# Two transformer layers with routed experts: the order of indirect transfers, of the ternary layer and of the experts' rows

## The reference

```python
x = x + L0_attn(layernorm(x))   # 16 heads of 16, rotary, causal window of 128, softmax, output projection
x = x + L0_ffn(layernorm(x))    # softmax router over 8 experts, the best 2 per token, renormalised gates;
                                # expert: silu(a) * b with (a, b) = x @ Wl1[e] + bl1[e] (512 + 512), then @ Wl2[e] + bl2[e]
x = x + L1_attn(layernorm(x))   # 16 heads, xpos rotation, biases, full causal softmax, output projection
x = x + L1_ffn(layernorm(x))    # ternary weight: clip(round(w / s), -1, 1) * s, s = mean(|w|)
```

## Time and profile before

| | us |
|---|---|
| median of three runs | 3257.35 |
| lowest, highest | 3247.95, 3259.71 |
| profiled execution, its own time | 3238.48 |
| its span | 3236.8 |
| PE busy | 2606.6 (81%) |
| DVE busy | 1855.1 (57%) |
| ACT busy | 1375.3 (42%) |
| POOL busy | 922.1 (28%) |
| mean granted clock | 0.900 of 2.4 GHz |

### The profile page before, as it was taken

How to read it: one execution, slowest core, us unless ns; L and a number is a source line. 1 busy time by engine, 2 the same in 40 slices (tenths; PEclk the granted TensorE clock), 3 DMA queues, 4 the chain that set the end, 5 groups by cost and what they waited for, 6 DMA issues and landing times. The chain is left out here.

```text
span 3236.8 us, 51965 instructions
## 1 busy us (share of the span) xinstructions
PE 2606.6 (81%) x17726; PEld 1745.3 (54%) x17726; DVE 1855.1 (57%) x6538; ACT 1375.3 (42%) x2419; POOL 922.1 (28%) x862
## 2 busy tenths in 40 slices
PE   3788888888888399989899952788888888888887
PEld 2455555555555277778777851344444444444444
DVE  3767766775675344444444443666666666666661
ACT  1445544554554233333333311255555545555554
POOL 2434544544342200000000004343333333334300
PEclk8889988988899699999999975799999989999998
DMA  4565565565433565566666544334444433333330
GB/s 118 164 199 169 190 202 166 166 210 194 145 126 99 186 239 212 214 217 215 214 214 214 215 137 117 102 102 123 131 120 128 122 106 106 106 105 111 100 93 14
DMA packets 263344, 494.65 MB, mean 153 GB/s; under 512 B 27104, under 2 KB 194272, under 8 KB 253024
## 3 DMA queue, kind: packets, MB, share of 16 engines
q1 hardware_dynamic: 245232, 437.99, 42.3%
q0 software_dynamic: 17904, 54.02, 5.0%
HBM read 302.53 MB, written 189.40 MB: 152 GB/s over the span
## 5 line engine op out<-in xcount | busy, mean ns | idle before, releaser
L882 DVE CUSTOM_DVE_ANT_0 a_junk<-a_bank,a_smask 128x256 bf16<-128x256 f32 (+3 forms) x2048 | 812.8, 435 | 499.5 <-PE a_bank L1073 477.2
L675 ACT ACTIVATE a_pr<-a_bank 128x512 f32<-128x512 f32 (+1 forms) x1152 | 635.7, 574 | 698.6 <-PE a_bank L994 636.3
L1073 PE MATMUL a_bank<-a_kst,a_qst 96*128 96x256 bf16 (+3 forms) x2048 | 464.8, 302 | 203.1 <-DVE a_nmax L882 149.6
L1095 PE MATMUL a_bank<-a_qst,a_kst 98*128 98x256 bf16 (+3 forms) x2048 | 440.4, 292 | 24.9 <-ACT a_pr L675 21.5
L1073 PEld LDWEIGHTS a_bank<-a_kst,a_qst 96*128 96x128 bf16 x2048 | 172.3, 102 | 457.9 <-DVE a_nmax L882 263.0
L1360 PE MATMUL e_bank<-e_xh,e_w 128*128 128x512 f32 x1248 | 402.9, 405 | 1.4 <-DVE e_xl L1341 1.4
L1113 PE MATMUL a_bank<-a_pr,a_va 128*32 128x256 f32 (+3 forms) x4096 | 365.9, 435 | 40.9 <-ACT a_pr L675 36.5
L994 PE MATMUL a_bank<-a_mask,a_identb 128*128 128x512 bf16 (+2 forms) x1152 | 356.1, 309 | 0.0
L1333 DVE SCALAR_TENSOR_TENSOR e_gf<-e_bank,e_b,e_sa 128x512 f32<-128x512 f32 x156 | 117.2, 751 | 280.5 <-ACT e_sa L1304 280.5
L1095 PEld LDWEIGHTS a_bank<-a_qst,a_kst 98*128 98x128 bf16 x2048 | 183.1, 101 | 152.5 <-ACT a_pr L675 72.0
L1304 ACT ACTIVATE e_sa<-e_bank,e_b 128x512 f32<-128x512 f32 x156 | 107.4, 689 | 371.5 <-PE e_bank L1360 371.3
(11 more groups left out here) (168 smaller groups left out, 4494.7 us busy)
## 6 DMA issues: line engine op xcount, KB each, us to landing
e_w<-ws_dram SPq DMA_DIRECT2D x39, 2048.0 KB, 9.5
a_parts_dram<-a_parts SPq DMA_DIRECT2D x224, 256.0 KB, 4.0
a_qst<-a_parts_dram SPq DMA_DIRECT2D x128, 384.0 KB, 9.9
a_kst<-a_parts_dram SPq DMA_DIRECT2D x128, 384.0 KB, 11.1
e_w<-ws_dram SPq DMA_DIRECT2D x39, 1024.0 KB, 6.0
a_parts_dram<-a_parts SPq DMA_DIRECT2D x32, 768.0 KB, 3.8
ws_dram<-a_ws SPq DMA_DIRECT2D x24, 1024.0 KB
e_xg<-xs SPq DMA_DIRECT2D x39, 512.0 KB, 6.0
```

Of the source, the lines that this page charges most:

```text
L675: nc.scalar.activation(pr[b][:, h:h + per, :], TB_[at % 2][:, 0:per * w].rearrange("p (h w) -> p h w", h=per), ACT.Exp, scale=scale).then_ ...
L882: last = nc.vector.tensor_tensor_reduce(junk[:, at % 2, j * w:(j + 1) * w], SB_[at % 2][:, j * w:(j + 1) * w], smask[:, T - w:T], scale=-1 ...
L1073: last = nc.tensor.matmul(out[:, j * w:(j + 1) * w], q[0:ROWS, hh, qb * P:(qb + 1) * P], k[0:ROWS, hh, k0:k0 + w], start=True, stop=True)
L1095: nc.tensor.matmul(out[:, j * w:(j + 1) * w], k[0:AUG, hh, b * P:(b + 1) * P], q[0:AUG, hh, q0:q0 + w], start=(j == 0), stop=False, skip_g ...
```

## The change

Six things are altered. (1) The indirect stores of layer 0 move by almost a turn: those of sequence r stood at 0.97 of turn r + 1 and now stand, one by one, at 0.115 to 0.213 of turn r + 2, each behind a wait for the last stack group of sequence r + 3; for that there is one turn more at the end. (2) The maxima go by one DMA from `nmt` straight into the stack, without DRAM; ACT's next copy waits for that landing. (3) Layer 1's gathers are issued singly, each behind its own tile's mix and with its own semaphore; gathers, mixes and statistics move forward, the statistics from the start of the next turn to 0.80 to 0.90 of the one before. (4) The ternary layer moves up, from 0.49 to 0.54 to 0.37 to 0.42, with the steps in front of it by 0.035 or less, and the next load from 0.55 to 0.435. (5) In layer 1 `norm`, `turn` and `project` are shifted. (6) The experts' rows of tile m + 1 are issued between the first and second weights of tile m; the loop's last two tiles are written out.

```diff
-    nmax_d = nc.dram_tensor(f"{name}_nmax_dram", [2, 2, H, T], BF16, kind="Internal").ap()
...
                     (0.145, ("add", o, 1))]
-            out += [(0.16 + 0.02 * t, ("stats2", o, t)) for t in range(NT)] + [(0.235, ("aggr2", o))]
+            if routed:
+                out += [(0.16 + 0.02 * t, ("stats2", o, t)) for t in range(NT)] + [(0.235, ("aggr2", o))]
+            else:
+                out += [(0.155 + 0.015 * t, ("stats2", o, t)) for t in range(NT)] + [(0.21, ("aggr2", o))]
             if routed:
...
                 out += [(0.15, ("y", o)), (0.50, ("turn2", o, 0)), (0.52, ("turn2", o, 1)), (0.58, ("score", o)),
-                        (0.66, ("exp2", o)), (0.79, ("place", o)), (0.97, ("scatter", o))]
+                        (0.66, ("exp2", o)), (0.79, ("place", o))]
                 out += [(0.615 + 0.0175 * k, ("gates", o, k)) for k in range(20)]
             else:
-                out += [(0.27 + 0.015 * t, ("norm2", o, t)) for t in range(NT)]
-                out += [(0.345, ("turn2", o, 0)), (0.36, ("turn2", o, 1)), (0.49, ("last", o, 0)), (0.51, ("last", o, 1)),
-                        (0.515, ("final", o, 0)), (0.535, ("final", o, 1)), (0.54, ("y", o))]
+                out += [(0.235 + 0.015 * t, ("norm2", o, t)) for t in range(NT)]
+                out += [(0.31, ("turn2", o, 0)), (0.325, ("turn2", o, 1)), (0.37, ("last", o, 0)), (0.385, ("last", o, 1)),
+                        (0.40, ("final", o, 0)), (0.415, ("final", o, 1)), (0.42, ("y", o))]
+        if routed and 0 <= i - 2 < B:
+            out += [(0.115 + 0.014 * k, ("scatter", i - 2, k)) for k in range(2 * NT)]
         if routed:
...
             out += [(0.01, ("v", s)), (0.035, ("vcopy", s, 0)), (0.055, ("vcopy", s, 1)), (0.54, ("minus", s, 0, 0)), (0.68, ("minus", s, 0, 1))]
-        for n, at in ((m, -0.5),) * (m == 0) + ((m + 1, 0.55),) * (0 <= m + 1 < B):
+        for n, at in ((m, -0.5),) * (m == 0) + ((m + 1, 0.55 if routed else 0.435),) * (0 <= m + 1 < B):
             out.append((at, ("load", n)))
             if mixed:
-                out += [(at - 0.2, ("gather", n, 0)), (at + 0.26, ("gather", n, 1))]
-                out += [(at + 0.19 + 0.02 * t, ("mix", n, 0, t)) for t in range(NT)]
-                out += [(at + 0.39 + 0.015 * t, ("mix", n, 1, t)) for t in range(NT)]
+                for t in range(NT):
+                    out += [(at - 0.165 + 0.025 * t, ("gather", n, 0, t)), (at + 0.125 + 0.02 * t, ("mix", n, 0, t)),
+                            (at + 0.135 + 0.025 * t, ("gather", n, 1, t)), (at + 0.285 + 0.02 * t, ("mix", n, 1, t)),
+                            (at + 0.365 + 0.02 * t, ("stats", n, t))]
+                out.append((at + 0.465, ("aggr", n)))
             else:
...
         if 0 <= m < B:
-            if mixed:
-                out += [(0.005 + 0.02 * t, ("stats", m, t)) for t in range(NT)] + [(0.075, ("aggr", m))]
-                out += [(0.125 + 0.015 * t, ("norm", m, t)) for t in range(NT)]
-            else:
-                out += [(0.03 + 0.02 * t, ("norm", m, t)) for t in range(NT)]
-            out += [(0.20, ("turn", m, 0)), (0.215, ("turn", m, 1))]
+            out += [(0.03 + 0.02 * t, ("norm", m, t)) for t in range(NT)]
+            out += [(0.18 if mixed else 0.20, ("turn", m, 0)), (0.195 if mixed else 0.215, ("turn", m, 1))]
             for a in range(2):
-                p = 0.27 + 0.13 * a
+                p = 0.24 + 0.19 * a if mixed else 0.27 + 0.13 * a
                 out += [(p, ("project", m, a)), (p + 0.04, ("rope", m, a, 0)), (p + 0.065, ("rope", m, a, 1)),
...
     order = []
-    for i in range(-2, B + 1):
+    for i in range(-2, B + 2):
         order += merged([turn(i)])
...
-        gathered = sem("gathered")
+        gathered = [sem(f"gathered{t}") for t in range(NT)]
...
                     sp.wait_ge(flip_free, flip_use[st] + 1)
-                    sp.dma_start(nmax_d[s % 2, half], nmt[half][:, :]).then_inc(nmax_stored, 16)
-                    sp.wait_ge(nmax_stored, 16 * (2 * s + half + 1))
-                    sp.dma_start(qst[s % 2][ROWS:AUG, half * H // 2:(half + 1) * H // 2, :],
-                                 nmax_d[s % 2, half].rearrange("(r h) n -> r h n", r=2))\
+                    sp.dma_start(qst[s % 2][ROWS:AUG, half * H // 2:(half + 1) * H // 2, :], nmt[half][:, :])\
                         .then_inc(nmax_loaded[s % 2][half], 16)
...
                 elif st[0] == "scatter":
-                    r = st[1]
+                    r, k, t = st[1], st[2] // NT, st[2] % NT
                     pool.wait_ge(rows_done, r + 1)
...
                         pool.wait_ge(padded, 16 * NE)
-                    for k in range(2):
-                        for t in range(NT):
-                            pool.indirect_dma_start(
-                                xs, bass.IndirectOffsetOnAxis(ap=row[r % 2][:, k, t:t + 1], axis=0),
-                                rn[r % 2][:, t, :], None).then_inc(scattered[r % 2], 16)
+                    if r + 3 < B:
+                        pool.wait_ge(stack_loaded[(r + 3) % 2][NG - 1], 32 * ((r + 3) // 2 + 1))
+                    pool.indirect_dma_start(
+                        xs, bass.IndirectOffsetOnAxis(ap=row[r % 2][:, k, t:t + 1], axis=0),
+                        rn[r % 2][:, t, :], None).then_inc(scattered[r % 2], 16)
                 elif st[0] == "gather":
-                    m, k = st[1:]
-                    pool.wait_ge(mixed_in, NT * (2 * m + k))
-                    for t in range(NT):
-                        pool.indirect_dma_start(
-                            yg[:, t, :], None, ys,
-                            bass.IndirectOffsetOnAxis(ap=yrow[:, k, m * NT + t:m * NT + t + 1], axis=0))\
-                            .then_inc(gathered, 16)
+                    m, k, t = st[1:]
+                    pool.wait_ge(mixed_in, max(0, NT * (2 * m + k - 1) + t + 1))
+                    pool.indirect_dma_start(
+                        yg[:, t, :], None, ys,
+                        bass.IndirectOffsetOnAxis(ap=yrow[:, k, m * NT + t:m * NT + t + 1], axis=0))\
+                        .then_inc(gathered[t], 16)
                 elif st[0] == "rope" and st[3] == 1:
...
                     act.wait_ge(flip_full, flip_use[st] + 1)
-                    act.wait_ge(nmax_stored, 16 * max(0, 2 * s + half - 1))
+                    if s:
+                        act.wait_ge(nmax_loaded[(s - 1) % 2][half], 16 * ((s - 1) // 2 + 1))
                     nc.scalar.copy(nmt[half][:, :], TRB[0:H, 0:T // 2].bitcast(BF16)).then_inc(flip_free, 1)
...
-                        dve.wait_ge(gathered, 16 * NT * (2 * m + k + 1))
+                    dve.wait_ge(gathered[t], 16 * (2 * m + k + 1))
...
     step(Seq(None, 1), Seq(None, 2))
-    with fori(1, (count - 1) // 2) as pair:
+    with fori(1, (count - 1) // 2 - 1) as pair:
         for c in range(2):
             step(Seq(pair, c), Seq(pair, c + 1))
+    for c in range(count - 3, count - 1):
+        step(Seq(None, c), Seq(None, c + 1))
     step(Seq(None, count - 1), None)
...
                         .then_inc(x_loaded, 16)
-                def weights_of(m, e):
+                def weights_of(m, e, between):
                     sp.wait_ge(ab_done, (m + -1).count(FC))
...
                     sp.dma_start(w[m.slot][:, :, 0:N1], ws_d[e][:, :, 0:N1]).then_inc(w1_loaded[m.slot], 16)
+                    if between:
+                        between()
                     sp.wait_ge(y_projected, (m + -1).count(2))
...
                     sp.dma_start(b2[m.slot][:, :], b2_d[e].partition_broadcast(P)).then_inc(b_loaded[m.slot], 16)
+                def expert_of(m):
+                    return sp.value_load(tab[0:1, 0, bass.ds(m.index(), 1)], min_val=0, max_val=NE - 1)
+
+                def row_of(m):
+                    return sp.value_load(tab[0:1, 1, bass.ds(m.index(), 1)], min_val=0, max_val=NE * REGION - TILE)
+
                 def step(s, m):
                     fresh(sp)
-                    if m:
-
-                        i = m.index()
-                        e = sp.value_load(tab[0:1, 0, bass.ds(i, 1)], min_val=0, max_val=NE - 1)
-                        r = sp.value_load(tab[0:1, 1, bass.ds(i, 1)], min_val=0, max_val=NE * REGION - TILE)
-                        if s:
-                            rows_of(m, r)
-                            weights_of(m, e)
-                        else:
-                            sp.dma_start(ident[:, :], ident_d).then_inc(const_loaded, 16)
-                            weights_of(m, e)
-                            for n in range(2):
-                                sp.wait_ge(scattered[n], 16 * 2 * NT * (B // 2))
-                            rows_of(m, r)
-                            sp.dma_start(gate_d, gate[:, :, :]).then_inc(kept_out, 16)
-                            sp.dma_start(yrow_d, yrow[:, :, :]).then_inc(kept_out, 16)
+                    if m and s:
+                        after = m + 1
```

(14 more changed lines are left out.)

1 line of the change is left out of this document (removed).

## The result

The changed kernel takes **3155.48 us** (median of four runs, 3151.46 to 3158.13) beside 3258.53 for the kernel before (four runs, 3247.95 to 3267.15): ratio 0.9684, 95% interval 0.9653 to 0.9715, so 103 us faster. I had said 2980 with a range of 2910 to 3100. The profiled execution of after took 3158.13 us with a span of 3156.5, 80 us less than the span before. The other 23 us lie in the two profiled executions: the one of before took 20 us less than the median of its kernel, the one of after 3 us more.

What follows compares the result with a forecast made beforehand. Three stages run one after another, PE the fullest engine in each, losing time to idleness and a low clock. Gains of 95 (first layer), 89 (experts) and 91 (second layer), 275 us, from 3257.35 gave 2982, stated as 2980, range 2910 to 3100.

Steps and rivals of the forecast that it cites:

- the stall needs both together: First layer, turn's end: PE stalls only when indirect stores meet stack transfers; separating them gains 13 x 7.3 = 95 us.
- The lower bound of 0 in the sum: First layer: the least gain from moving the stores, 0 us, if the freeze goes with them.
- 0 to 3 us late per turn for ACT's normalisation: First layer: POOL, held by the added stack wait, reaches L550 0 to 3 us late; nothing counted on the path.
- the rival: First-layer paragraph: the stores carry the stall along, no gain there, 3077 us, chance 0.13; second-layer paragraph: the second rival.
- the price of the removed wait: Second layer: ending DVE's wait for the second gather gains 6.5 us a turn, 14 x 6.5 = 91 us.
- My lower bound, 42: Second layer: the least gain from the moved load, gathers and mixes, 14 x 3 = 42 us.
- Both rivals: First and second layer both gain nothing, only the experts gain: 3257 - 89 = 3168 us, chance 0.04.
- the second rival: Second layer only changes its wait: x late, POOL held, parts, stacks and gathers pile up; gain 0, 3073 us, chance 0.12.

Runs made afterwards that it cites:

- x7: The changed kernel with the indirect stores left out, the experts reading other rows of the same size; 3059.07 us.
- x8: The changed kernel with each indirect store replaced by a plain POOL store of the same rows to its own tensor; 3061.06 us.
- y1: The changed kernel unaltered, on a third chip where the kernel before took 3170.30 us; 3070.88 us, ratio 0.9693.
- y4: The changed kernel without the wait for the stack's last group ahead of the stores, on the chip of y1; 3058.95 us, ratio 0.9649.
- x2_stores: The kernel before with only the indirect stores moved to 0.115 to 0.213 of the next turn, behind the last stack group; 3229.32 us, ratio 1.0171.
- x6: The changed kernel with POOL's second-layer bias add moved from 0.50 to 0.76 of a turn; 3143.07 us, ratio 0.9663.
- z3: The changed kernel with the stores back at 0.97 of a turn and the second-layer bias add at 0.76; 3134.53 us, ratio 0.9616.
- x3_second: The kernel before with only the second layer's part (ternary layer, load, gathers, mixes, statistics, projections moved); 3164.13 us, ratio 0.9965.
- x4_three: The changed kernel with the eight indirect stores put back at 0.97 of a turn, without their wait; 3057.53 us, ratio 0.9626.
- x1_experts: The kernel before with only the experts' part, the next tile's rows issued earlier; 3075.47 us, ratio 0.9681.
- groups 2, 4 and 5: Three groups of follow-up runs, each on one chip, where the kernel before took 3254.41, 3260.43 and 3259.11 us.
- groups 1 and 3: Two groups of follow-up runs, each on one chip, where the kernel before took 3173.02 and 3170.30 us.

## Why the prediction was wrong

**The experts: right.** 89 us were forecast, a tile of 17.5, and clock 1.00; the tile is 17.34 and 36 tiles gave 94 us. The rows' wait is gone and the clock no longer falls.

**The first layer: the step that failed is "the stall needs both together".** I took the freeze for a collision of the stores with the stacks' loads and removed it by keeping them apart, 13 x 7.3 = 95 us. The stores do it without the stacks. After shows it with a DMA share of 0.40, and on a chip with the freeze x7 and x8 price stores and freeze together at 96 us: 12 of these also stand on a chip without it (y1 against x7), and 85 are the freeze (3155 against 3071). So the size was about right and the owner wrong. The contrast I leaned on (1035 to 1044 in rows 3, one turn) was a single case, and not a clean one: in that burst too PE's increments due at 1043.68 and 1044.12 came at 1045.10 and 1045.17. The freeze was there, and little of PE's work waited on it; why it was shorter stays open. Nor does the full DMA share at the old place start the freeze sooner: of PE's increments due 2.5 to 5 us after a burst's first store 16 of 48 are on time (within 0.15 us) in before and 12 of 44 in after, and of those due 5 to 7.5 us after it 0 of 13 and 1 of 48. The table's later stop at the new place is PE's supply of work that is already released. From the first turn to the last (114.9 to 1050.5, against 117.1 to 1035.8) after is 17 us longer than before: the freeze is still there, now beside the projection, and the held stores cost some 12 of it (y1 against y4). The lower bound of 0 in the sum didn't hold either.

**A second step that failed there is a term put at nothing:** "0 to 3 us late per turn for ACT's normalisation, of which I count nothing on the path, since its transposes stand at 0.50". ACT works in order, and the exponentials that PE needs stand behind that normalisation. Without the straight copy of the maxima the held stores cost up to 56 us (x2_stores), with it 12 (y1 against y4).

The rule of the Trainium skill that I set beside the rival ("SBUF — State Buffer", section "Who interferes with whom": a DMA never contends with a compute engine) gave the right time for this layer, nothing gained. But a burst of indirect stores issued by POOL did hold up the compute engines on some chips, as far as the events tell by their increments and not by their access to SBUF.

**The second layer: the step that failed is the price of the removed wait.** DVE's 7.4 us a turn were not on the path alone. The wait went as forecast (96.1 to 0.0), yet the turn stayed: 74.0 to 74.4 in the two profiles, 74.5 to 74.4 on one chip. By the traces two things took its place, and the rival named neither: the mixes now run beside POOL's two-input operations (0.48 us each before, 0.75 now, 30 us in all, and the subtraction of L892, L894 before, from 27.8 to 32.1), and PE waits for the maxima in the middle of the turn (its weight loads 142.0 to 192.6, 51 us in 13 turns; the products' waits lie within these). At 2617.6 to 2635.5 DVE is busy 17.14 of 17.90 us, and the clock falls behind it:

```profile
2617.60:2635.50 17.90, 11.11 (x77) 4.49 (x76) 17.14 (x44) 9.54 (x15) 12.74 (x9) 0.79 0.43 134
2628.00:2638.30 10.30, 7.45 (x34) 3.18 (x35) 7.87 (x21) 4.22 (x7) 8.18 (x6) 0.50 0.14 41
```

So a gap at one place of DVE's turn became a full stretch at another. Of this only the bias add's part was tested (x6 and z3, 12 us each); that the rest explains the lost gain is argued. By itself (x3_second) the part brought 9 us where 91 were in the sum. My lower bound, 42, counted only the wait and never the place where the work went.

**The chances.** "Both rivals" gave 3168 with a chance of 0.04, and that is where the result lies, though the second rival's mechanism (parts, stacks and gathers piling up) was not what happened. 0.04 is little more than two unrelated accidents give (0.17 x 0.16 = 0.03), though both terms rested on the same habit: to price a removed wait in full. The gain is the experts' on a chip without the freeze too (3170 to 3071), where there was no stall to keep or to remove; that part of the forecast could not have come true there by any order of the stores.

**The maxima** were costed at nothing, and no run tested them alone. With the stores at their old place SP's 128.3 us of waiting are gone without a trace in the turns; x4_three less x1_experts less x3_second leaves 3173 - 3057.5 - 97.5 - 8.9 = 9 us for them and for the parts' interplay. With the stores behind the stack wait they were worth 3.6 us a turn (61.5 in x2_stores, 57.9 in y1_after).

## What to carry to other kernels

Before moving transfers apart, take each of them out once: one run without the stores would have shown their owner. Run the kernel before on the same chip beside every variant. On a chip that shows the freeze, break bursts of indirect stores into pieces of four or less that truly lie apart in time, and check on the timeline that they do not follow one another all the same. When a wait on one engine goes, look at what its work will run beside, and price the gain as zero until the next bound is named. When you add a wait to an in-order queue, follow what stands behind it in that queue, and behind that in the next engine's.

## What the runs showed of the hardware that I had not expected

On the chips of groups 2, 4 and 5 and in the first comparison, indirect stores issued in a row by POOL (128 rows of 1 KB, 1.27 us apart) held up the semaphore increments of PE by up to 6 us, from 2.5 to 5 us after the first store (the third or fourth) until soon after the last; those of DVE and ACT are mostly missing from the trace in the same stretches. Plain DMAs from the same queue with the same bytes did not do it (3061 against 3155, and no increment off). The indirect loads of the second layer did it in small: in before, in thirteen turns, 128 of 1632 increments of PE, 52 of 1034 of DVE and 23 of 903 of ACT are off by over 0.15 us, each within 2 us of such a load's issue, and 60 events come 0.15 to 0.86 us behind the last work that can have given them; the others aren't in the trace. On the chip of x1_experts, with the same loads, none is off, and the turns are no shorter there (74.5 against 74.0).

What the stores cost over the first layer on such a chip, each sum set against the 3059 of x7: 17 us with one burst of four in a turn, about 30 with two (3077 + 12 - 3059), 63 with six and two, and 87 to 96 with eight. These sums hold what the stores' places cost without the freeze too, which is known only for eight in a row: nothing at the old place, 12 at the new one.

Whether it shows in full is a matter of the chip or of something that stays the same during a group of runs: the same kernel took 3071 and 3155 us, another 3057, 3058 and 3146, and the kernel before 3170 and 3173 or 3254 to 3260. All seven kernels of groups 1 and 3 whose stores stood in a row have at most four increments off in the first layer, x2_stores among them, and every kernel of groups 2, 4 and 5 with indirect stores has tens. What differs between the chips isn't in the traces, and I leave it open.
